# Attention row maxima in one-bank pieces, one key difference rectified on ScalarE, a new order of the matmuls in a turn, and loops written out

## The reference, cut to what matters

```python
xn = layernorm(x)                                   # x: 2 x 4096 x 256
q, k, v = split(xn @ W_qkv + b_qkv)                 # 16 heads of 16 dimensions
attention = softmax(q @ k.T, axis=-1) @ v           # each head: 4096 x 4096 scores
h = butterfly(xn @ W_exp + b_exp, up_weights)       # 1024 wide, 10 stages
h = butterfly(gelu(h + up_bias), down_weights)
out = x + attention + (h @ W_con + b_con + down_bias)
```

## Time and profile before

| | |
|---|---|
| median of 3 runs | 6314.39 us (6313.53 to 6325.08) |
| profiled execution, its own time | 6311.6 us |
| its span, first to last instruction | 6309.5 us |
| PE, DVE, ACT, POOL busy | 6081.0, 5228.2, 4511.0, 438.2 us |
| mean granted TensorE clock | 0.966 of full speed |

### The profile page before, as it was taken

The page is one execution under the profiler, slowest core; times in us unless marked ns, Lnnn a source line. Parts: engine busy times, 40 slices in busy tenths (PEclk is TensorE's granted clock), DMA queues, the critical chain, the costliest instruction groups (busy, mean ns, idle before and its releaser), DMA issues. The chain is left out here.

```text
span 6309.5 us, 114675 instructions
## 1 busy us (share of the span) xinstructions
PE 6081.0 (96%) x35808; PEld 2576.8 (41%) x35808; DVE 5228.2 (83%) x5128; ACT 4511.0 (71%) x8581; POOL 438.2 (7%) x354
## 2 busy tenths in 40 slices
PE   8699999999999999999999999999999999999999
PEld 5333333333333333333333333333333333333498
DVE  6788898989899898989898898989898988996133
ACT  3177777777777777777777777777777777777444
POOL 2499200000000000000000000000000000000000
PEclk9699999999999999999999999999999999999699
DMA  8512000000000000000000000000000000000011
GB/s 290 153 52 78 25 17 15 18 19 18 16 10 18 19 18 19 16 16 18 19 18 14 11 18 19 18 18 14 18 18 19 16 13 14 18 18 1 18 49 40
DMA packets 229722, 193.65 MB, mean 31 GB/s; under 512 B 171112, under 2 KB 191976, under 8 KB 217320
## 3 DMA queue, kind: packets, MB, share of 16 engines
q1 hardware_dynamic: 225648, 162.76, 9.0%
q0 software_dynamic: 3456, 23.07, 1.1%
HBM read 124.92 MB, written 58.72 MB: 29 GB/s over the span
## 5 line engine op out<-in xcount | busy, mean ns | idle before, releaser
L573 DVE TENSOR_REDUCE maxima<-psum 128x1 f32<-128x1024 f32 x4096 | 4834.9, 1219 | 605.7 <-PE psum L665 592.4
L559 ACT ACTIVATE probs<-psum 128x512 f32<-128x512 f32 x8192 | 4243.0, 603 | 1411.2 <-PE psum L682 1410.4
L682 PE MATMUL psum<-q_rows,k_rows 50*128 50x512 f32 x8192 | 3049.5, 453 | 77.4 <-ACT probs L559 41.5
L665 PE MATMUL psum<-k_rows,q_rows 48*128 48x512 f32 x8192 | 2499.4, 456 | 89.7 <-DVE maxima L573 87.3
L682 PEld LDWEIGHTS psum<-q_rows,k_rows 50*128 50x128 f32 x8192 | 1392.4, 189 | 2725.5 <-ACT probs L559 2473.9
L693 PE MATMUL psum<-probs,v_cols 128*32 128x512 f32 x16384 | 2239.9, 619 | 0.7 <-ACT probs L559 0.7
L665 PEld LDWEIGHTS psum<-k_rows,q_rows 48*128 48x128 f32 x8192 | 1028.1, 189 | 279.7 <-DVE maxima L573 196.9
L693 PEld LDWEIGHTS psum<-probs,v_cols 128*32 128x32 f32 x16384 | 326.1, 109 | 530.9 <-ACT probs L559 318.3
L904 ACT ACTIVATE gelus<-psum,bias_up 128x512 f32<-128x512 f32 x128 | 88.3, 690 | 189.3 <-PE psum L868 187.6
L946 DVE TENSOR_TENSOR hidden_low<-gelus,hidden_high 128x512 fp32r<-128x512 f32 x128 | 88.7, 693 | 100.8 <-ACT hidden_high L907 100.8
L613 DVE STREAM_TRANSPOSE o_t<-psum 128x512 f32<-128x512 f32 x64 | 45.4, 709 | 141.6 <-PE psum L693 141.6
(11 more groups left out here) (79 smaller groups left out, 1344.8 us busy)
## 6 DMA issues: line engine op xcount, KB each, us to landing
q_rows<-q_parts SPq DMA_DIRECT2D x128, 256.0 KB
q_parts<-parts SPq DMA_DIRECT2D x32, 512.0 KB, 5.5
k_parts<-parts SPq DMA_DIRECT2D x32, 512.0 KB, 3.6
k_rows<-k_parts SPq DMA_DIRECT2D x64, 256.0 KB
q_rows<-q_parts SPq DMA_DIRECT2D x128, 128.0 KB
planes<-in_up_planes POOLq DMA_DIRECT2D x10, 1024.0 KB, 5.1
planes<-in_down_planes POOLq DMA_DIRECT2D x10, 1024.0 KB, 5.1
y<-in_x SPq DMA_DIRECT2D x16, 512.0 KB, 5.3
```

The source lines that it names most:

```text
L559: nc.scalar.activation(probs[:, (2 * u + half) % 4, BANK * g:BANK * g + BANK], ps_s[:, score_bank(c, e), :], ACT.Exp).then_inc(s_exp, 1)
L573: nc.vector.tensor_reduce(maxima[:, parity, n:n + 1], ps_max[slot].rearrange("p a b -> p (a b)"), axis=AX_X, op=ALU.max).then_inc(s_region ...
L665: return nc.tensor.matmul(ps_max[slot][:, half, :], q_rows[c][lower:lower + ROWS, P * t:P * t + P], k_rows[c // 2][lower:lower + ROWS, key ...
L682: nc.tensor.matmul(ps_s[:, score_bank(c, e), :], k_rows[c // 2][lower:lower + ROWS + MAX_PARTS, P * u:P * u + P], q_rows[c][lower:lower + ...
```

## The change

The three PSUM areas of the attention change: 4 banks for scores, 3 single banks for regions, 1 for the sums. A region becomes 8 *pieces* of 512 keys for each query tile. Piece 3 of a tile is a matmul with `k_diff`, the difference between the keys of chunk 6 and chunk 7; ScalarE rectifies its result into `spill` (max(a, b) = b + relu(a - b)). For piece 6 (chunk 7) VectorE then adds `spill` and takes the maximum in one `tensor_tensor_reduce`; the other six pieces have a 512-wide `tensor_reduce` each. The difference is multiplied one tile ahead. `k_diff` is made in the preparation (chunks 6, 7, 14 and 15), stored to DRAM in two parts and loaded with two more DMAs for each head.

In the diff, `PIECE` and `SCORE` give (half, key chunk) of each piece and (half, query group) of each score. TensorE's order in a turn (one unit: 7 or 8 pieces of tile u + 21, 8 scores of unit u + 1, 2 sums of unit u) is new, scores run a unit ahead of the sums that use them, and score banks are taken back after four. The scale and the add at the end of a superblock go to POOL, whose weight folding is cut into 36 operations for each superblock. All attention and preparation loops are written out.

```diff
-    REGIONS = QT * N // (2 * BANK)
+    AHEAD = QT + 5
+    COLUMNS = PIECES - 1
+    WEIGHT_OPS = 36
-        def chunk_loop(engine, step):
-            with engine.Fori(1, CHUNKS // 2 - 2) as i:
+        def chunk_loop(step):
+            for c in range(CHUNKS):
+                step(c, c // 2, c % 2, min(c, 2), CHUNKS - c)
...
-        ps_max = [psum[:, 0:2, :], psum[:, 2:4, :]]
-        ps_s = psum[:, 4:7, :]
+        ps_s = psum[:, 0:4, :]
+        ps_max = psum[:, 4:7, :]
         ps_o = psum[:, 7, :]
+        PIECE = [(1, 0), (1, 1), (0, 0), (1, 2), (0, 1), (0, 2), (1, 3), (0, 3)]
+        DIFFERENCE, MERGED = 3, 6
+        SCORE = [(r // 2 % 2, 2 * (r // 4) + r % 2) for r in range(2 * QG)]
...
+                for s in range(SUPER):
+                    for k in range(WEIGHT_OPS * s, min(WEIGHT_OPS * s + WEIGHT_OPS, 6 * len(rows_of_turns))):
+                        fold_weights(k)
+                    scale_and_add(s)
...
+                def rectify(n):
+                    act.wait_ge(s_diff_ps, n + 1)
+                    if n >= 2:
+                        act.wait_ge(s_region_free, vector_uses[use_of[n - 2, MERGED]])
+                    nc.scalar.activation(spill[:, n % 2, :], region(use_of[n, DIFFERENCE]), ACT.Relu).then_inc(s_spilled, 1)
+                for u in range(UNITS_ALL):
+                    if u + 1 < UNITS_ALL:
+                        for r in range(QG):
+                            exp(u + 1, r)
+                    if u + AHEAD + 1 < TILES_ALL:
+                        rectify(u + AHEAD + 1)
+                    if u + 1 < UNITS_ALL:
+                        for r in range(QG, 2 * QG):
+                            exp(u + 1, r)
...
+                def reduce_piece(n, j):
+                    if j == MERGED:
+                        dve.wait_ge(s_spilled, n + 1)
+                        dve.wait_ge(s_region, vector_uses[use])
+                        nc.vector.tensor_tensor_reduce(merged[:, :], region(use), spill[:, n % 2, :], 1.0, LOWEST,
+                                                       ALU.add, ALU.max, accum_out=largest).then_inc(s_region_free, 1)
+                    else:
+                        dve.wait_ge(s_region, vector_uses[use])
+                        nc.vector.tensor_reduce(largest, region(use), axis=AX_X, op=ALU.max).then_inc(s_region_free, 1)
...
+                def free_region(use):
+                    if use >= 3 and by_vector[use - 3]:
+                        pe.wait_ge(s_region_free, vector_uses[use - 3])
+                    if use >= 3 and by_scalar[use - 3]:
+                        pe.wait_ge(s_spilled, scalar_uses[use - 3])
...
+                    if e >= 4:
+                        pe.wait_ge(s_exp, e - 3)
...
+                for u in range(UNITS_ALL):
+                    n = u + AHEAD
+                    if n % QT == TURN_TILE and n // QT <= SUPER:
+                        neg_to_rows(n // QT - 1)
+                    piece(n, 0)
+                    score(u + 1, 0)
+                    piece(n, 1)
+                    score(u + 1, 1)
+                    score(u + 1, 2)
+                    piece(n, 2)
+                    score(u + 1, 3)
+                    sums(u, 0)
+                    piece(n, 3)
+                    piece(n, 4)
+                    score(u + 1, 4)
+                    score(u + 1, 5)
+                    piece(n, 5)
+                    score(u + 1, 6)
+                    score(u + 1, 7)
+                    piece(n, 6)
+                    piece(n, 7)
+                    sums(u, 1)
```

More of the change, by code:

```diff
@@ L430, in attention_and_butterfly_ffn @@
         FIN = 3
-        EVAC = 3
-        def superblocks(engine, step):
-            with engine.Fori(0, SUPER // 4 - 1) as i:
-                for c in range(4):
-                    step(4 * i + c, c, i, False)
-            i = SUPER // 4 - 1
-            for c in range(4):
-                step(4 * i + c, c, i, True)
         def wait_for_stores(engine):
@@ L562, in _, with exp @@
-                superblocks(act, step)
+                def exp(u, r):
+                    half, g = SCORE[r]
+                    if g == 0 and u >= 2:
+                        act.wait_ge(s_pv, 2 * (u - 2) + half + 1)
+                    act.wait_ge(s_score, 2 * QG * u + r + 1)
+                    nc.scalar.activation(probs[:, 2 * (u % 2) + half, BANK * g:BANK * g + BANK],
+                                         ps_s[:, r % 4, :], ACT.Exp).then_inc(s_exp, 1)
+                def rectify(n):
[3 more added lines that the diff above has]
+                    nc.scalar.activation(spill[:, n % 2, :], region(use_of[n, DIFFERENCE]), ACT.Relu).then_inc(s_spilled, 1)
@@ new lines, in piece @@
+                def piece(n, j):
+                    if j == DIFFERENCE:
+                        n += 1
+                    if n >= TILES_ALL:
+                        return
+                    m, t = divmod(n, QT)
+                    if t == 0 and j == DIFFERENCE:
+                        pe.wait_ge(s_q[m % 4], 16 * LOADS * (m // 4 + 1))
+                        pe.wait_ge(s_k[m // 2 % 2], 16 * K_LOADS * (m // 4 + 1))
+                    half, chunk = PIECE[j]
+                    lower, at = HALF_P * half, m // 2 % 2
+                    keys = k_diff[at] if j == DIFFERENCE else k_rows[at][:, BANK * chunk:BANK * chunk + BANK]
+                    free_region(use_of[n, j])
+                    nc.tensor.matmul(region(use_of[n, j]), q_rows[m % 4][lower:lower + ROWS, P * t:P * t + P],
+                                     keys[lower:lower + ROWS, :], start=True, stop=True)\
+                      .then_inc(s_diff_ps if j == DIFFERENCE else s_region, 1)
@@ L715, in _ @@
+                for n in range(AHEAD):
+                    if n == QT + TURN_TILE:
+                        neg_to_rows(0)
+                    for j in range(PIECES):
+                        piece(n, j)
+                    if n == AHEAD - 2:
                         pe.wait_ge(s_ones_in, 16 * 4)
-                        for e in range(3):
-                            score(0, 0, e, first=True)
+                        for r in range(QG):
+                            score(0, r)
+                for r in range(QG, 2 * QG):
+                    score(0, r)
```

427 lines of the change are left out of this document (208 added, 219 removed).

## The result

The changed kernel takes 5698.82 us (median, 5698.62 to 5700.97), the kernel before 6313.96 beside it (6310.81 to 6325.08): a ratio of 0.9024, with a 95% interval of 0.9008 to 0.9039. The profiled execution took 5699.03 us, its span 5697.2. The forecast was 5612; 87 us were to be explained.

What follows compares the result with a forecast made beforehand. It took a chain through ScalarE's exponentials, 2.61 us per half turn, as the bound. Head 323, 1003 turns of 4.81 (4824), tail 83 and 377 behind it gave a span of 5607, forecast 5612 us, range 5500 to 6020.

Steps and rivals of the forecast that it cites:

- The chain of 2.62: Half turn before: score to ScalarE, two exps, sums to next score: 0.53 + 0.49 + 0.60 + 1.00 us.
- PE's turn, 4.72: TensorE's new order laid out by matmul starts: 2.59 us behind sums(u, 0) and 2.13 behind sums(u, 1).
- only p2 is late: Region banks: of the pieces, only p2 waits for its bank (p7's reduction), by 0.1 us.
- Meetings and once-a-superblock work, 0.09 a turn: Meetings of the three queues plus TensorE's transposes of maxima and sums add 0.09 us to the turn, giving 4.81.
- ACT and DVE hidden: Per turn, ScalarE's 4.41 us and VectorE's 4.45 us lie hidden under TensorE's 4.72.
- Weight loads: Rival: loads wait within one array half, steps 0.40 not 0.23 us, turn 5.83, time 6635 us; chance 4%.
- Table reloads: Rival: ScalarE reloads its table for Relu and Exp, ACT's turn 6.98 us, time about 7800; chance 2%.
- Loops written out, 130 us: Attention loop: 15 loop ends of 8.7 us each go, contained in counting every turn at 4.81.
- that is gone: The VectorE scale's stall beside POOL's folding, 4.04 us instead of 0.41, ends as scale and add move to POOL.
- Head, 323: Time to the first turn: first reduction at 225.1, plus 5, 21 tiles of 4.34 = 91, plus 2 us.
- Tail, 83 at full clock: Last 21 turns, without pieces, at 3.95 us each and 2.4 GHz; the lower clock would add about 57 us.
- Behind the tail, 377: After attention: 381 us before, less 5 for the FFN's first matmuls, plus 1 for POOL's last operation.

Runs made afterwards that it cites:

- last experiment: The kernel before with each exponential over 256 of its 512 columns: 5934.26 us, ratio 0.9399.
- both cuts: The changed kernel with ScalarE's rectification and VectorE's reduction of p4 each over 64 of 512 columns: 5498.54 us, ratio 0.8712 to the kernel before.

## Why the prediction was right, and where its numbers were off

**What bounded the kernel before.** Right. The chain of 2.62 was the bound, though no engine in it was full: shortening ScalarE's two operations in it took the half turn to VectorE's 2.4 (last experiment).

**The chain is gone, and each engine's own work sets the turn.** Half right. The sums no longer wait behind fresh exponentials and the turn fell from 5.22 to 4.87. But no engine's own work sets it. VectorE has seven operations of 0.61, 4.25, ScalarE nine, 4.4, and the matmul queue 4.63 with both cuts, or 4.49 by its two halves where each was free of waits (2.37 and 2.12). What sets the longer half is a round trip of one PSUM bank: sums, p4, its reduction, p7, sums.

**PE's turn, 4.72.** The half behind `sums(u, 1)` was laid out at 2.13 and measured 2.12 to 2.14. The half behind `sums(u, 0)` was laid out at 2.59 and measured 2.74. Two errors of unlike sign stand in it. I took matmuls of the two halves as pairs in the order of the queue. They run further ahead, so that the half without waits is 2.37, near 1.00 + 0.34 + 3 x 0.23 + 0.33 = 2.36. And I wrote that "only p2 is late". p7 is: VectorE begins p4's reduction at 3005.27, 0.56 behind p4's start, and lets the bank go after 0.69, not after 0.61. The 0.61 is the distance between two starts; a bank is free at the end. With the 0.06 to the next matmul that makes p7 possible 1.31 behind p4, where my layout had it at 1.26 (0.34 + 4 x 0.23). Behind such a wait the sums come 0.43 later, not the 0.33 that I took. 1.00 + 0.56 + 0.69 + 0.06 + 0.43 = 2.74. Against my layout 0.05 + 0.10 = 0.15 is missing, and it was within reach of the earlier trace rows, which has the 0.43 behind a score that waited.

**Meetings and once-a-superblock work, 0.09 a turn.** Too much by itself: the superblock of 78.1 less 16 x 4.86 leaves 0.3, or 0.02 a turn, most of it in the half where the transposed maxima pass (2.36 in place of 2.12) and in the one behind the sums' transpose (2.86 in place of 2.74). So 4.72 + 0.15 + 0.02 = 4.89 is to be set against the 78.1 / 16 = 4.88 that was measured and the 4.81 forecast; 1003 x 0.07 = 70 of the 87 us.

**"p6 waits for the rectification; ACT gets there before s7 is through".** The trace shows p6 waiting 0.38 in nearly every turn, and cutting the rectification changed nothing. As a description it was wrong, as a cost of nothing it was right. The wait shows because the queue arrives there earlier than in my layout, with time that it then loses at p7 in any case.

**ACT and DVE hidden.** Right: rectification 0.60 alone and 0.49 to the next start (3005.24 to 3005.73). The merged operation was taken at 0.68 from start to start and is 0.61, its 0.68 being its duration.

The Trainium skill's Vector Engine (DVE) Microarchitecture Reference, section "Points that are easy to get wrong", gives half rate to such operations with two non-bf16 SBUF sources and an accumulator. With one source in PSUM the 0.61 here is that of a plain reduction, so this case does not fall under it, and no run here has two SBUF sources and an accumulator.

**Weight loads.** Not a cost: matmuls of one half still start 0.23 or 0.24 apart (s4, s5 and p5 of the first half begin within 0.47, from 3005.05 to 3005.52 in the turn shown) and the turn of 5.83 did not come. The rule that the prediction cited from TensorE: Matmul & The Clock Gate, "The mechanism" of Part 3, of the Trainium skill, is contradicted by the changed kernel's trace as by that of before.

**Table reloads.** None between Relu and Exp: the changed kernel's trace has one table load in the attention.

**Loops written out, 130 us.** 108 by themselves in the kernel before.

**POOL.** Right that it costs little: "that is gone" held for the stall of 4.04, which came back as 3.79 when the add went back to VectorE. The 69 us of that run are not a saving on the kernel before, which had the stall twice.

**Head, 323.** 331.5, 8 us more. The first reduction came at 231.2, 1 us late (230). The 21 tiles ahead, 5 us of it, took about 4.6 each and not 4.34, with VectorE idle for 0.29 behind the difference in each while the granted clock was 0.50:

```profile
283.12 0.60 ACT L635 ACTIVATE spill<-psum 128x512 f32<-128x512 f32 x1 [3.98 <-PE psum L746]
283.72 1.29 DVE L669 TENSOR_REDUCE maxima<-psum 128x1 f32<-128x512 f32 x2 [0.29 <-PE psum L746]
```

**Tail, 83 at full clock.** The clock was right: 1.00 to 5315, where the kernel before had 0.50. The turns took 4.14, not 3.95, 4 us in all.

**Behind the tail, 377.** 5697.2 - 5313.3 = 383.9, 7 us more. The 5 us taken off did not come: the FFN's first matmuls ran at a granted clock of 0.50 again.

```profile
5317.00:5336.00 19.00, 11.72 (x42) 10.13 (x43) 9.85 (x22) 4.78 (x6) 0.00 (x0) 0.50 0.28 84
```

And the first of them starts 4.9 behind the last transpose of the sums, where it was 2.3 in the kernel before. POOL's scale and add (0.62 and 0.72) now stand there and end 2.4 ahead of that matmul; what fills the rest no row says. The 1 us put on for POOL was 2.7. The median lies 1.6 above the span, not 4.9, which gives 3 back.

Of the 87 us, then, 70 are the turn, 8 the head, 4 the tail, 7 what stands behind it, less 3 for the step from span to median.

**What the parts are worth.** Undone one at a time: the difference on ScalarE 560 us, the fourth score bank 1222 (62 of it the clock of the tail), the scale on POOL 69; the loop alone in the kernel before 108. These are far more than 615 together, so they do not add up: the new order costs time without the fourth bank, and does little without the difference on ScalarE.

## What to carry to other kernels

Lay out the round trip of each buffer as well as each engine's work: from the start that fills it to the end that frees it, and on to what the last waiter delays. Use durations to the end for it and starts for throughput. A wait that the profile puts at hundreds of us can be worth nothing when another wait stands right behind it, and a name in the waits can stand beside time that is no wait at all; cut the releaser short and see. An order that runs further ahead is worth only what the buffers behind it allow: this one lost to the old one with three score banks and beat it by 10% with four.

## What the runs showed of the hardware

Matmuls for different halves of the array overlapped beyond the neighbour in the queue: with both cuts nine of them took 1.38 us to the sums, where pairing them in order gives 1.59. A merged add with maximum over 512 columns, one source in PSUM, took 0.68 us and let the next operation start after 0.61, the same as a plain reduction, with 0.08 of accumulator reading hidden. Beside POOL's folding, operations of VectorE that read PSUM kept their 0.67 and 0.68, while an add between two SBUF tiles took 3.79 and one without folding beside it 0.41. Relu and Exp alternated on ScalarE at 0.49 from start to start, with no table load between them. And the granted clock stayed at 1.00 (2.4 GHz) through the tail, where the kernel before fell to 0.50 (1.2 GHz) after PE had been busy for 16.74 of 20 us; the run with three score banks fell too, and its tail took 62 us longer.
